# Attention with a packed V, the sums of exponentials on GpSimd, and row maxima over two PSUM banks at a time

## The reference

```
nx = rmsnorm(X, g1)
Q  = nx @ Wq.T  (4 heads of 64);   Kc = nx @ Wkc.T, Vc = nx @ Wvc.T  (one head of 64, shared)
scores = Q Kc^T / sqrt(64);  attn = softmax(scores)          # 2048 x 2048 for each of 2 x 4 heads
X = X + (attn @ Vc) @ Wo.T
h = rmsnorm(X, g2); router logits, top 2 of 8 experts; X + shared(h) + sum of gate * expert(h)
```

## Time and profile before

| | |
|---|---|
| median of three runs | 1458.81 us |
| the profiled execution | 1461.01 us, its span 1459.0 us |
| first exponential of the loop | 235.16 us into the span |
| PE busy | 1307.4 us (90%) |
| DVE busy | 1079.0 us (74%) |
| ACT busy | 893.1 us (61%) |
| POOL busy | 385.4 us (26%) |

### The profile page before, as it was taken

How to read it: one execution, slowest core, us unless ns; L and a number is a source line. 1 busy time by engine, 2 the same in 40 slices (tenths; PEclk the granted TensorE clock), 3 DMA queues, 4 the chain that set the end, 5 groups by cost and what they waited for, 6 DMA issues and landing times.

```text
span 1459.0 us, 19334 instructions
## 1 busy us (share of the span) xinstructions
PE 1307.4 (90%) x6008; PEld 920.7 (63%) x6008; DVE 1079.0 (74%) x2143; ACT 893.1 (61%) x1450; POOL 385.4 (26%) x282
## 2 busy tenths in 40 slices
PE   4777677999999999999998999999997999999994
PEld 2334545665666665676665666666664797887774
DVE  4956987777887777777885877787974867546778
ACT  2355564776766766666686766666675856555551
POOL 0443431222311212211111311111154001623346
PEclk9989797999999999999999999999998999999998
DMA  5001016200000000000000001000011323555634
GB/s 196 1 1 44 15 58 208 81 1 1 1 1 1 1 1 1 1 1 1 1 1 1 1 1 44 1 0 1 22 51 65 104 93 117 195 148 165 191 115 149
DMA packets 56418, 75.82 MB, mean 52 GB/s; under 512 B 8383, under 2 KB 48063, under 8 KB 56064
## 3 DMA queue, kind: packets, MB, share of 16 engines
q1 hardware_dynamic: 36030, 46.29, 9.7%
q0 software_dynamic: 6144, 16.79, 3.7%
q10 hardware_dynamic: 14146, 11.52, 2.3%
HBM read 37.27 MB, written 37.22 MB: 51 GB/s over the span
## 4 chain that ended last, share of the span: by engine, by line
PE 63%; DVE 19%; issue 5%; ACT 5%; POOL 5%; DMA 1%; ACTq 1%; POOLq 0%; DVEq 0%; SPq 0%
PE PS L1802 8%; PE PS L1700 6%; PE PS L1749 6%; PE PS L1732 6%; PE PS L1751 6%; PE PS L1735 6%; PE PS L1750 6%; DVE mx L1159 5%; PE PS L1828 4%; DVE PL L1189 4%; PE PS L1713 3%; POOL y L1534 2%; PE PS L1686 2%; POOL xbuf L1522 2%; PE PS L1786 1%
## 5 line engine op out<-in xcount | busy, mean ns | idle before, releaser
L1159 DVE TENSOR_REDUCE mx<-PS 128x1 f32<-128x512 f32 x512 | 344.1, 686 | 100.6 <-PE PS L1700 98.5
L770 ACT ACTIVATE PT<-PS 128x1024 f32<-128x1024 f32 x256 | 262.8, 1027 | 231.8 <-PE PS L1735 221.8
L1514 POOL TENSOR_TENSOR PL<-PT,PH 128x1024 fp32r<-128x1024 f32 x61 | 146.2, 2396 | 541.8 <-ACT PH L775 530.1
L775 ACT ACTIVATE PH<-PT 128x1024 fp32r<-128x1024 f32 x256 | 271.2, 1060 | 8.1
L1189 DVE TENSOR_TENSOR PL<-PT,PH 128x1024 fp32r<-128x1024 f32 x195 | 238.9, 1225 | 44.4 <-ACT PH L775 43.8
L1749 PE MATMUL PS<-PH,VH 128*65 128x512 f32 x512 | 219.6, 429 | 8.6 <-DVE PL L1189 8.6
L1751 PE MATMUL PS<-PL,VH 128*65 128x512 f32 x512 | 202.9, 396 | 0.0
L1750 PE MATMUL PS<-PH,VL 128*65 128x512 f32 x512 | 202.3, 395 | 0.0
L1700 PE MATMUL PS<-KA,Q 128*128 128x512 f32 x384 | 161.1, 432 | 16.9 <-DVE mx L1159 12.1
L1732 PE MATMUL PS<-Q,KA 128*128 128x512 f32 x384 | 128.0, 415 | 2.5 <-POOL KB L1491 2.5
L1735 PE MATMUL PS<-Q,KB 65*128 65x512 f32 x384 | 122.6, 401 | 0.0
(11 more groups left out here) (239 smaller groups left out, 2486.5 us busy)
## 6 DMA issues: line engine op xcount, KB each, us to landing
xbuf<-xT SPq DMA_DIRECT2D x26, 384.0 KB, 4.4
xg<-xbuf SPq DMA_DIRECT2D x78, 128.0 KB, 2.3
ybuf<-yo ACTq DMA_DIRECT2D x78, 128.0 KB
nxT<-in_wexp SPq DMA_DIRECT2D x9, 768.0 KB, 4.4
x<-in_x SPq DMA_DIRECT2D x8, 512.0 KB, 11.9
x_scratch<-x SPq DMA_DIRECT2D x2, 2048.0 KB, 6.9
nxT<-x_scratch SPq DMA_DIRECT2D x32, 128.0 KB
out<-X SPq DMA_DIRECT2D x32, 128.0 KB, 1.9
```

The source lines that it names most:

```text
L770: act.activation(PT[:, gs % 2, :], PS[:, bk:bk + 2, :].rearrange("p a n -> p (a n)"), ACT.Exp, scale=0.125).then_inc(sem("pt"), 1)
L775: act.activation(PH[:, gs % 3, :], PT[:, gs % 2, :], ACT.Copy).then_inc(sem("pt_h"), 1)
L1159: dve.tensor_reduce(mx[:, half, i, c:c + 1], PS[:, k, :], AX, ALU.max).then_inc(sem("dve_out"), 1)
L1514: pool.tensor_tensor(PL[:, gs % 3, :], PT[:, gs % 2, :], phf[:, gs % 3, :], ALU.subtract).then_inc(sem("pl_g"), 1)
```

## The change

Four things change in the loop.

1. V is packed: `V[:, t, 0, :]` is the high part and `V[:, t, 1, :]` the low part, and one matmul with all 128 columns gives VH by PH in partitions 0 to 63 and VL by PH in 64 to 127. With the matmul for PL that makes two matmuls instead of three for each half. The ones column is gone. `O` has 128 partitions and 1024 columns, and the projection's weight stands twice in `woa`, once for each half of the partitions, so that the projection's matmul adds the two.
2. The sums: GpSimd adds each step's `PT` into `Z` (`total`, every step; a copy where the key tile is 0), 1024 columns. A job `z_mm` then multiplies `Z` by a column of ones (eight matmuls of one column), and VectorE takes the reciprocals of all eight at once. The reciprocal in each `proj` is gone.
3. The low part is VectorE's in every step, with two buffers of `PL` instead of three, and `exp(gs)` now waits for both `low(gs - 2)` and `total(gs - 2)`.
4. The maxima: `max_mm` computes two matmuls into banks 6 and 7 as a pair and VectorE reduces 1024 scores at once. A pair always begins at bank 6.

The projection of the first half of a head now runs in the second half of the same head, that of the second half in the head after, so the tail has eight tiles of it instead of sixteen.

```
 def max_jobs(bh, half):
-    return ([("max_mm", bh, half, i, c) for i in range(8) for c in range(4)]
+    return ([("max_mm", bh, half, i, c) for i in range(8) for c in range(2)]
...
-        if bh > 0:
-            m, e = (30, 60) if bh == 4 else (49, 92)
-            todo += spread(proj_jobs(bh - 1)[:8], 4, m) + spread(proj_jobs(bh - 1)[8:], m + 1, e)
+        todo += [(50, ("z_mm", bh, 0))] + spread(proj_jobs(bh, 0), 53, 92)
+        if bh > 0:
+            todo += [(3, ("z_mm", bh - 1, 1))] + spread(proj_jobs(bh - 1, 1), 5, 46)
...
             if gs >= 2:
-                low_done(w, gs - 2)
+                w.wait_ge(sem("pl"), gs - 1)
+                w.wait_ge(sem("z"), gs - 1)
             act.activation(PT[:, gs % 2, :], PS[:, bk:bk + 2, :].rearrange("p a n -> p (a n)"), ACT.Exp,
...
         def max_mm(bh, half, i, c):
             k = banks.bank["max_mm", bh, half, i, c, 0]
             pe_of(w, ("max_mm", bh, half, i, c, 0))
-            dve.tensor_reduce(mx[:, half, i, c:c + 1], PS[:, k, :], AX, ALU.max).then_inc(sem("dve_out"), 1)
+            dve.tensor_reduce(mx[:, half, i, c:c + 1], PS[:, k:k + 2, :].rearrange("p a n -> p (a n)"), AX, ALU.max).then_inc(sem("dve_out"), 1)
...
-            if gs >= 3:
-                w.wait_ge(sem("av"), 2 * (gs - 2))
-            dve.tensor_tensor(PL[:, gs % 3, :], PT[:, gs % 2, :], phf[:, gs % 3, :], ALU.subtract).then_inc(sem("pl_v"), 1)
+            if gs >= 2:
+                w.wait_ge(sem("av"), 2 * (gs - 1))
+            dve.tensor_tensor(PL[:, gs % 2, :], PT[:, gs % 2, :], phf[:, gs % 3, :], ALU.subtract).then_inc(sem("pl"), 1)
...
+        def total(gs):
+
+            g, kc = divmod(gs, 16)
+            w.wait_ge(sem("pt"), gs + 1)
+            if kc == 0:
...
+                pool.tensor_copy(Z[:, g % 2, :], PT[:, gs % 2, :]).then_inc(sem("z"), 1)
+            else:
+                after_last("z")
+                pool.tensor_tensor(Z[:, g % 2, :], Z[:, g % 2, :], PT[:, gs % 2, :], ALU.add).then_inc(sem("z"), 1)
...
         for gs in range(NGS):
-            if by_pool(gs):
-                low(gs)
+            total(gs)
...
+            if kc < 15:
+                pe.matmul(PS[:, 4 + n, :], V[:, t, :, :].rearrange("p a d -> p (a d)"), PH[:, gs % 3, c], start=(kc == 0),
+                          stop=False)
+                pe.matmul(PS[0:64, 4 + n, :], V[:, t, 0, :], PL[:, gs % 2, c], start=False, stop=False).then_inc(sem("av"), 1)
```

More of the change, by code:

```diff
@@ L94, in __init__, with add_pair @@
         self.bank, self.pe, self.out, self.prev, self.held = {}, {}, {}, {}, {}
+    def add_pair(self, job, ring):
+        self.turn += self.turn % 2
+        self.n += 1
+        self.count["v"] += 1
+        for k in range(2):
+            b, key = ring[self.turn % len(ring)], (*job, k)
+            self.turn += 1
+            self.bank[key], self.pe[key] = b, self.n
+            self.prev[key] = self.held.get(b)
+            self.out[key] = self.held[b] = ("v", self.count["v"])
     def add(self, job, ring):
+        if READERS.get(job[0]) == "vv":
+            return self.add_pair(job, ring)
         for k, reader in enumerate(READERS.get(job[0], "")):
@@ L127, in q_jobs, with proj_jobs @@
     return [(n, b, pair, c) for c in range(4) for n in ("q_mm", "q_hi", "q_lo")]
-def proj_jobs(bh):
-    return [("proj", bh, i) for i in range(NT)]
+def proj_jobs(bh, qc):
+    return [("proj", bh, 8 * qc + i) for i in range(8)]
 def norm_jobs(b):
@@ L215, in tail_order @@
     norm = norm_jobs(1)
-    last = [x for j, p in enumerate(proj_jobs(7)) for x in (p, norm[j])] + [norm[NT]]
+    last = [("z_mm", 7, 1)] + [x for j, p in enumerate(proj_jobs(7, 1)) for x in (norm[j], p)] + norm[8:]
     side = [(-2, 9, last),
@@ L231, in tail_order @@
     return {s: flat(v) for s, v in order.items()}
[L234 to L240, removed]
 class Once:
@@ L341, in _build @@
     c3 = ExitStack()
-    VH = sb("VH", [P, NB * NT, 65], F32R, c=c3)
-    VL = sb("VL", [P, NB * NT, 65], F32R, c=c3)
-    mx = sb("mx", [P, 2, 8, 4], c=c3)
+    V = sb("V", [P, NB * NT, 2, 64], F32R, c=c3)
+    mx = sb("mx", [P, 2, 8, 2], c=c3)
     m16 = sb("m16", [P, 2, 8], c=c3)
     mT = sb("mT", [8, 2, P], F32R, c=c3)
-    rz = sb("rz", [P, 2, 1], c=c3)
+    rz = sb("rz", [P, 2, 8], c=c3)
+    ones = sb("ones", [P, 1], c=c3)
     wk = sb("wk", [P, 2, P], c=c3)
@@ L396, in _build @@
     PH = sb("PH", [P, 3, 1024], F32R, c=c3)
-    PL = sb("PL", [P, 3, 1024], F32R, c=c3)
-    O = sb("O", [65, S], c=c3)
-    woa = sb("woa", [65, 4, 257], c=c3)
+    PL = sb("PL", [P, 2, 1024], F32R, c=c3)
+    Z = sb("Z", [P, 2, 1024], c=c3)
+    O = sb("O", [P, 1024], c=c3)
+    woa = sb("woa", [P, 4, D], c=c3)
     QA = [Q01[0][:, :], Q01[1][:, :], QA2[:, :]]
@@ L403, in _build @@
     qaf = [q.bitcast(F32) for q in QA]
-    vhf = VH[:, :, :].bitcast(F32)
+    vf = V[:, :, :, :].bitcast(F32)
     phf = PH[:, :, :].bitcast(F32)
@@ L620, in _ @@
         front_done(w)
-        sp.dma_start(woa[:, :, :], I["woA"]).then_inc(sem("d_woa"), 16)
+        for a in (0, 64):
+            sp.dma_start(woa[a:a + 64, :, :], I["woA"][0:64, :, 0:D]).then_inc(sem("d_woa"), 16)
         w.wait_ge(sem("zero"), 1)
@@ L1170, in max_turn, with z_mm @@
             dve.tensor_copy(mT[:, half, :], PS[0:8, k, 0:P]).then_inc(sem("dve_out"), 1)
+        def z_mm(bh, qc):
+            k = banks.bank["z_mm", bh, qc, 0]
+            pe_of(w, ("z_mm", bh, qc, 0))
+            if bh:
+                out_of(w, ("proj", bh - 1, 8 * qc + 7, 0))
+            dve.reciprocal(rz[:, qc, :], PS[:, k, 0:8]).then_inc(sem("dve_out"), 1)
         def proj(bh, i):
-            b, s, k = bh // 4, i % 2, banks.bank["proj", bh, i, 0]
-            n = b * NT + i
+            b, k = bh // 4, banks.bank["proj", bh, i, 0]
+            n, qc = b * NT + i, i // 8
             pe_of(w, ("proj", bh, i, 0))
-            mark(dve.reciprocal(rz[:, s, :], PS[:, k, 256:257]))
-            w.wait_ge(own, made[0])
+            out_of(w, ("z_mm", bh, qc, 0))
             if bh % 4:
                 out_of(w, ("proj", bh - 1, i, 0))
-            dve.scalar_tensor_tensor(X2[:, n, :], PS[:, k, 0:256], rz[:, s, :], X2[:, n, :], ALU.mult,
+            dve.scalar_tensor_tensor(X2[:, n, :], PS[:, k, 0:256], rz[:, qc, i % 8:i % 8 + 1], X2[:, n, :], ALU.mult,
                                      ALU.add).then_inc(sem("dve_out"), 1)
@@ L1425, in _ @@
         for gs in range(NGS):
-            if not by_pool(gs):
-                low(gs)
+            low(gs)
             for part in range(3):
@@ L1696, in max_mm @@
             q_dup(bh, 2 * half + i // 4)
-            out_of(w, ("k_mm", b, c, 0))
-            k = bank("max_mm", bh, half, i, c, 0)
             q0 = (8 * half + i) * P
-            pe.matmul(PS[:, k, :], QA[bh % 3][:, q0:q0 + P], KA[b][:, c * 512:c * 512 + 512], start=True,
-                      stop=True).then_inc(sem("pe_use"), 1)
+            for j in range(2):
+                n = 2 * c + j
+                out_of(w, ("k_mm", b, n, 0))
+                k = bank("max_mm", bh, half, i, c, j)
+                mm = pe.matmul(PS[:, k, :], QA[bh % 3][:, q0:q0 + P], KA[b][:, n * 512:n * 512 + 512], start=True, stop=True)
+            mm.then_inc(sem("pe_use"), 1)
         def max_turn(bh, half):
@@ L1709, in proj, with z_mm @@
             qc, n = divmod(i, 8)
-            w.wait_ge(sem("d_woa"), 16)
+            w.wait_ge(sem("d_woa"), 32)
+            q0 = n * P
             w.wait_ge(sem("o"), 4 * bh + 2 * qc + n // 4 + 1)
             k = bank("proj", bh, i, 0)
-            pe.matmul(PS[:, k, 0:257], O[0:65, i * P:i * P + P], woa[0:65, bh % 4, :], start=True,
+            pe.matmul(PS[:, k, 0:D], O[:, q0:q0 + P], woa[:, bh % 4, :], start=True,
                       stop=True).then_inc(sem("pe_use"), 1)
+        def z_mm(bh, qc):
+            w.wait_ge(sem("ones"), 1)
+            w.wait_ge(sem("z"), 16 * (2 * bh + qc + 1))
+            k = bank("z_mm", bh, qc, 0)
+            for i in range(8):
+                mm = pe.matmul(PS[:, k, i:i + 1], Z[:, qc, i * P:i * P + P], ones[:, :], start=True, stop=True)
+            mm.then_inc(sem("pe_use"), 1)
         def qk(gs):
@@ L1748, in av @@
                 w.wait_ge(sem("o"), 4 * bh + 2 * qc + n - 1)
-            pe.matmul(PS[0:65, 4 + n, :], VH[:, t, :], PH[:, r, c], start=(kc == 0), stop=False)
-            pe.matmul(PS[0:65, 4 + n, :], VL[:, t, :], PH[:, r, c], start=False, stop=False)
-            pe.matmul(PS[0:65, 4 + n, :], VH[:, t, :], PL[:, r, c], start=False, stop=(kc == 15)).then_inc(sem("av"), 1)
+            if kc < 15:
+                pe.matmul(PS[:, 4 + n, :], V[:, t, :, :].rearrange("p a d -> p (a d)"), PH[:, gs % 3, c], start=(kc == 0),
+                          stop=False)
+                pe.matmul(PS[0:64, 4 + n, :], V[:, t, 0, :], PL[:, gs % 2, c], start=False, stop=False).then_inc(sem("av"), 1)
+            else:
+                pe.matmul(PS[0:64, 4 + n, :], V[:, t, 0, :], PL[:, gs % 2, c], start=False, stop=False)
```

(2 more changed lines are left out.)

69 lines of the change are left out of this document (29 added, 40 removed), and 4 rows, old and new, of the table READERS.

## The result

The changed kernel takes 1858.6 us (median of four runs, 1852.9 to 1864.3) against 1460.8 us before: a ratio of 1.272, 95% interval 1.265 to 1.279. It is 398 us slower; 160 were forecast. The span of the profiled execution is 1858.0 us.

| us | before | after |
|---|---|---|
| until exponential 0 | 235.2 | 233.9 |
| exponentials 0 to 244 | 835.2 | 1207.1 |
| exponentials 244 to 255 | 36.9 | 65.8 |
| from exponential 255 to the end | 351.7 | 351.1 |

A forecast was written before the change was run, and what follows sets the result against it. TensorE was taken to set the 3.42 us step, GpSimd's indirect DMAs the loop's end. Terms -19 + 18 + 98 + 29 + 8 + 32 - 1 - 5 = +160 gave 1619 us, range 1490 to 1735.

The forecast's parts named there:

- three signs of being wrong: In the loop: low part stays at 1.22 us, loop under 3.3 us a step, or ACT still waits for PE.
- The maxima: 32 front instructions become 16, -1 us; in the loop, DVE time lying beside POOL's, without a price.
- POOL's sum: First 244 steps: POOL's addition and DVE's low part exclude each other, at least 3.345 us a step, -19.0 us.
- missed turns: 244 loop steps: DVE returns after POOL began another addition; 82 misses at 1.2 us, +98, bounds 0 and 215.
- the other holders: 244 loop steps: casts, L1153 subtractions and scalings also hold the port, 37.5 us, less copies at key tiles 0: +18.
- the clock: Loop: missed turns stop PE long enough to lower its clock; 41 x 0.7 us, +29, between 0 and 126.
- the router's steps: Steps 230 to 243: some 45 small DVE instructions may each meet an addition; +8 us, from 0 to 32.
- Packed V at nothing: Loop: two of six av matmuls go, 0.46 us of PE a step, worth nothing where something else takes longer.
- The last 12 steps: End of loop: POOL's 32 indirect DMAs plus 12 additions, together 75 us against 41.9 before; +32 us.
- A (turns hold): Loop: DVE's work between low parts always fits in 2.26 us, PE at full clock; 1492 us, chance 0.18.
- B (the wrong turn sticks): Loop: DVE too late in every step with a reduction, 215 replaces 98, clock goes along; 1736 us, chance 0.24.
- C (no exclusion): Loop: the two engines don't exclude each other, some 2.8 us a step; about 1335 us, chance 0.05.

The follow-up runs named there:

- b: The changed kernel with maxima over 512 scores again, in banks 6 and 7 in turn as before: 1.162 of the kernel before, loop 1122.2 us.
- c: The changed kernel with maxima over 512 scores again and GpSimd's sums over only 128 of 1024 columns: 1.000 of the kernel before, loop 883.6 us.
- i: b with GpSimd's additions over 512 of the 1024 columns: 1.038 of the kernel before, loop 935.7 us.
- g: c with low parts on GpSimd in every fourth step and three buffers of PL, as before: 1.004 of the kernel before.
- f: b with the exponential written back into PSUM, VectorE's low part reading PSUM and PH, GpSimd summing PH: 1.084 of the kernel before, loop 990.2 us.
- e: The kernel before with all side jobs of the loop in bank 6 alone, maxima still over 512 scores: 1.196 of the kernel before.

## Why the prediction was wrong

The direction and the exclusion were right, the size was off by 238 us, and one of the three signs of being wrong that the prediction named came true (ScalarE still waits for PE). In the first 244 steps the pair costs 154 us (after - `b`) that had been priced at nothing, and the additions cost 219.5 (`b` - `c`) where the terms for them come to 134. These two are the miss. By the prediction's own steps:

- *The maxima* ("in the loop they are DVE time that lies beside POOL's"): this step failed. The reduction was sized right (1.22 us, 1.220 measured). The handover, 0.73 us, was nearly right at full clock (median 0.82 between two reductions of `after`) and too low at 1.2 GHz (1.31). But I put both into VectorE's time only. I gave no price to TensorE, whose matmuls come in the program's order and which has both side banks taken: 151 us of loop (after - `b`), 155 to 167 alone. No rival held it.
- *POOL's sum, its missed turns, the other holders, the clock and the router's steps*: together +134 in the first 244 steps; `b` against `c` gives 1053.3 - 833.8 = 219.5, 86 more. Which of the five terms fell short isn't shown. The floor of 3.345 us a step wasn't what bound: over the loop the port is held some 240 x 2.26 + 256 x 1.085 + 52 (copies and other holders) = 872 of 1273 us, and `i` pays without a floor. The path was another: a late low part delays the reductions behind it, these TensorE, and TensorE the scores. From `c` to `b` TensorE's wait for the reductions ahead of its maxima (weight loads) grows from 70.7 to 138.4 us, and ScalarE's for the scores from 215.1 to 320.3.
- *Which wait ends last*: I expected ScalarE to be released by POOL or DVE, no longer by PE, and named the opposite as what would prove me wrong. It is so: 417.9 us for PE in the 244 steps, 57.2 for POOL and DVE together. The low parts' mean is 1.75 us where I wrote over 2, the additions' 2.68 (2.4 to 3.5 forecast), PE is busy 74% (under 75%).
- *Packed V at nothing*: right, but not by the cause given. I let the port hide it. `g` brings 5 us in 244 steps with the port nearly free, its short additions and `z_mm` included.
- *The clock* (+29, up to 126): 0.84 in the loop, 0.97 in `c`. A mean of 0.84 means that about a third of the 1208 us ran at 1.2 GHz. How much of the 401 us it caused wasn't separated, since it falls wherever TensorE waits.
- *The last 12 steps* +32 (its terms give 33): measured 28.9. Here the mechanism holds: the same sum with a short addition, 44.2 + 12 x (0.56 + 0.16) = 52.8, fits the 51.6 of `g`. *Front* -1: -1.3. *Tail* -5: -0.7.
- *Rivals*: A (turns hold) and B (the wrong turn sticks) both priced the port only. C (no exclusion) is refuted by `f` and `b` together. B says that the clock goes with the missed turns but adds nothing for it; with the 126 us that the prediction gives as the clock's bound, its top would have been 1833, still under what was measured, and all of it put down to the port and the clock.

The common fault is the reading of the earlier trace rows. PE at 805 of 835 us looked like a TensorE whose matmuls set the step, so that 0.46 us less of them would be slack for everything else. By `g`, taking 0.46 us of matmuls out of a step of 3.42 wins 0.02; by `e`, taking one of two side banks costs 20%. What set the step was already, at least in part, TensorE's order through the side banks. A row that hints at it stood in front of me: VectorE idle for 98.5 us until L1700 had filled a bank, on an engine with work to do.

## What to carry to other kernels

Two buffers that are filled and emptied by different engines are a double buffer only if they can be held one at a time: one instruction that reads both makes them one, and saving its fixed cost (here 33 us of VectorE) cost 151 to 178 us. When an engine looks 96% busy, test it by taking work away before giving its slack a value. Before work is put on GpSimd in every step, count VectorE's instructions with two inputs in SBUF: in these traces each of them and GpSimd's take turns (and a scaling with one, 0.353 us, once took 2.483). And look at what else stands in GpSimd's order: behind the scatters even short additions cost some 13 to 15 us (`c`, `g`).

## What the runs showed of the hardware

- A VectorE subtraction with one input in PSUM and one in SBUF isn't held by GpSimd's additions: 256 low parts of 1.178 to 1.226 us beside 240 additions (`f`), and 1.178 to 3.631 with both inputs in SBUF (`b`).
- ScalarE can write its exponential back into the PSUM banks it reads: 1.009 us for 1024 columns against 1.027 into SBUF.
- A reduction over 1024 columns across two PSUM banks takes 1.220 us, two of 512 take 2 x 0.686.
- TensorE's granted clock was 1.00 at 1005 us, fell to 0.50 by 1007, after stops of 2.65 and 1.32 us, and stayed there through three turns of 2.54 us with 1.32 idle in each (`after`, 1007 to 1015).
